# A vision tower kernel on one core: three matmul groups and two element-wise steps change their place within the round

## What is computed

```python
h = einsum(patches, W)                                   # 768 -> 256, the tokens
n = layernorm(h)
x_proj = n @ in_w + in_b
mod = gelu(n @ mod_w1 + mod_b1) @ mod_w2 + mod_b2        # 256 -> 1024 -> 256
y = irfft(rfft(x_proj * mod) * rfft(kernel))             # circular convolution over the 196 tokens
h = h + y @ out_w + out_b
n = layernorm(h)
gate = top 2 of softmax(n @ router_W.T + router_b)       # 6 experts, renormalised
h = h + n @ base_W.T + base_b + (n @ A.T) @ B.T + sum_e gate_e (n @ routed_A_e.T) @ routed_B_e.T
```

## Time and profile before

| | |
|---|---|
| median of 3 runs | 1248.16 us (1247.44 to 1250.17) |
| the profiled execution | 1247.64 us |
| its span in the trace | 1245.8 us |
| PE busy | 1223.9 us (98%) |
| DVE busy | 888.8 us (71%) |
| ACT busy | 643.2 us (52%) |
| POOL busy | 406.9 us (33%) |
| granted TensorE clock | 0.999 of full speed |

### The profile page before, as it was taken

The page is one execution under the profiler, slowest core; times in us unless marked ns, Lnnn a source line. Parts: engine busy times, 40 slices in busy tenths (PEclk is TensorE's granted clock), DMA queues, the critical chain, the costliest instruction groups (busy, mean ns, idle before and its releaser), DMA issues.

```text
span 1245.8 us, 20849 instructions
## 1 busy us (share of the span) xinstructions
PE 1223.9 (98%) x7914; PEld 1175.7 (94%) x7914; DVE 888.8 (71%) x2591; ACT 643.2 (52%) x1197; POOL 406.9 (33%) x459
## 2 busy tenths in 40 slices
PE   9999999999999999999999999999999999999998
PEld 8899999999999999999999999999999999999996
DVE  6477766677766777766777666777667777667777
ACT  6645555545555445555455555455554445454432
POOL 3523244332244232343232443323442323433220
PEclk9999999999999999999999999999999999999999
DMA  7310222221322111222202222212221112211001
GB/s 244 94 49 20 68 69 68 56 34 47 69 69 68 56 28 55 69 68 56 59 23 68 69 68 56 33 49 68 68 69 55 26 57 68 68 56 33 14 13 34
DMA packets 85089, 72.97 MB, mean 59 GB/s; under 512 B 64775, under 2 KB 78958, under 8 KB 81150
## 3 DMA queue, kind: packets, MB, share of 16 engines
q1 hardware_dynamic: 84990, 71.66, 20.4%
HBM read 43.07 MB, written 12.85 MB: 45 GB/s over the span
## 4 chain that ended last, share of the span: by engine, by line
PE 80%; DVE 9%; ACT 7%; issue 2%; DMA 1%; SPq 1%; POOL 0%; ACTq 0%; DVEq 0%
PE rotating L1457 16%; PE rotating L1458 15%; PE rotating L1459 15%; PE rows_ps L1457 8%; PE rows_ps L1458 6%; PE rows_ps L1459 6%; PE turn L1744 5%; PE turn L1507 2%; PE rows_ps L1517 2%; ACT gelu_h L661 2%; DVE y_l L1161 1%; ACT y_h L698 1%; ACT gelu L656 1%; DVE gelu_l L1106 1%; DVE gated_l L1186 1%
## 5 line engine op out<-in xcount | busy, mean ns | idle before, releaser
L529 POOL TENSOR_TENSOR folded<-modulated 128x196 f32<-128x196 f32 x63 | 38.1, 605 | 565.0 <-DVE modulated L1118 565.0
L656 ACT ACTIVATE gelu<-rotating,consts 128x392 f32<-128x392 f32 x256 | 145.4, 582 | 109.2 <-PE rotating L1459 108.9
L514 POOL TENSOR_TENSOR gelu_l<-gelu,gelu_h 128x784 fp32r<-128x784 f32 x62 | 128.7, 2075 | 213.1 <-DVE norm L1101 172.0
L509 POOL TENSOR_TENSOR patches_l<-patches,patches_h 128x384 fp32r<-128x384 f32 (+1 forms) x186 | 182.1, 1008 | 2.8 <-ACT patches_h L608 2.8
L1457 PE MATMUL rotating<-x_h,w_h 128*128 128x392 f32 x512 | 177.2, 346 | 1.6 <-ACT gelu L656 1.6
L1457 PE MATMUL rotating<-gelu_h,w_h 128*128 128x392 f32 x512 | 177.4, 346 | 0.0
L1458 PE MATMUL rotating<-x_l,w_h 128*128 128x392 f32 x512 | 174.6, 341 | 0.0
L1459 PE MATMUL rotating<-x_h,w_l 128*128 128x392 f32 x512 | 174.6, 341 | 0.0
L1458 PE MATMUL rotating<-gelu_l,w_h 128*128 128x392 f32 x512 | 174.2, 340 | 0.0
L1459 PE MATMUL rotating<-gelu_h,w_l 128*128 128x392 f32 x512 | 174.0, 340 | 0.0
L1457 PE MATMUL rows_ps<-tokw_h,patches_h 128*128 128x256 f32 x570 | 162.9, 286 | 1.5 <-DVE patches_l L871 1.5
(11 more groups left out here) (300 smaller groups left out, 2997.7 us busy)
## 6 DMA issues: line engine op xcount, KB each, us to landing
patches<-dram_x_rest SPq DMA_DIRECT2D x30, 1152.0 KB, 5.2
out<-h_sb SPq DMA_DIRECT2D x30, 384.0 KB, 2.5
prod<-spec_y SPq DMA_TRANSPOSE x60, 3.2
patches<-dram_x_first SPq DMA_DIRECT2D x2, 384.0 KB, 5.7
h_sb<-dram_x_second SPq DMA_DIRECT2D x1, 768.0 KB, 7.6
patches<-dram_x_fourth SPq DMA_DIRECT2D x1, 768.0 KB, 9.6
h_sb<-dram_first SPq DMA_DIRECT2D x2, 320.0 KB, 3.5
gelu<-dram_w SPq DMA_DIRECT2D x1, 512.0 KB, 8.1
```

Of the source, the lines that this page charges most:

```text
L509: pool.tensor_tensor(patches_l[:, k, 0:n], patches[:, k, 0:n], patches_h[:, k, 0:n].bitcast(F32), ALU.subtract).then_inc(pool_patches_lo, 1)
L514: pool.tensor_tensor(gelu_l[:, 2 * j:2 * j + 2, :], gelu[:, 2 * j:2 * j + 2, :], gelu_h[:, 2 * j:2 * j + 2, :].bitcast(F32), ALU.subtract)\
L529: pool.tensor_tensor(folded[:, m, 0, :, 1:NF], fwd, back, ALU.add)
L656: act.activation(gelu[:, k, :], bank(g + 1, UP[k])[:, 0:GT], ACT.Gelu, bias=b1_bias[:, k:k + 1]).then_inc(act_gelu, 1)
```

## The change

Four edits, all of order; no instruction is added, removed or resized.

1. PE: `routed(tail)` goes from between up blocks 6 and 7 to behind up block 7.
2. ACT: `gelu_tile(mid, 5)` goes from behind `fold_hi` to ahead of `gated_hi`.
3. DVE: `gelu_lo(mid, 2)` goes from ahead of the spectral products to behind `spectrum_of_y`, where `gelu_lo(mid, 3)` follows it.
4. PE: the first of the eight blocks of `mlp_down(mid, 0)` goes from behind the mixer's products to ahead of them, with the wait for gelu 6 (`act_gelu`) that stood before it.

```diff
@@ ACT
                 gelu_tile(mid, 4)
+                gelu_tile(mid, 5)
                 if in_range(tail):
                     gated_hi(tail, bank(i, TURN_GATED))
                 if in_range(back):
                     fold_hi(back)
-                gelu_tile(mid, 5)
                 gelu_hi(mid, 1)
@@ DVE
                     finish(tail, rows_ps)
-                for j in range(0 if i == 1 else 2, 3):
-                    gelu_lo(mid, j)
                 if in_range(back):
                     real_products(back)
                     imaginary_products(back)
                     spectrum_of_y(back)
-                gelu_lo(mid, 3)
+                for j in range(0 if i == 1 else 2, 4):
+                    gelu_lo(mid, j)
@@ PE
                 mlp_up(mid, 6)
+                pe.wait_ge(act_gelu, HC * mid + 6)
+                mlp_up(mid, 7)
                 if in_range(tail):
                     routed(tail, rows_ps)
-                pe.wait_ge(act_gelu, HC * mid + 6)
-                mlp_up(mid, 7)
                 if in_range(back):
                     dft(back)
@@ PE
+                pe.wait_ge(act_gelu, HC * mid + 7)
+                mlp_down(mid, 0, (0,))
                 if in_range(back):
                     pe.wait_ge(dve_y_lo, DH * back + DH)
                     mixer_tiles(back, rows_ps[:, 2], bank(i, OUT)[:, 0:DIM])
-                pe.wait_ge(act_gelu, HC * mid + 7)
-                mlp_down(mid, 0, range(HC))
+                mlp_down(mid, 0, range(1, HC))
```

## The result

The changed kernel takes 1216.88 us (median of 4 runs, 1213.93 to 1218.77) where the kernel before takes 1248.21 us: ratio 0.9745, 95% interval 0.9718 to 0.9771. Measured again in a later session, it took 1214.24 us (1214.13 to 1214.35) against 1247.59: 0.9728 (0.9715 to 0.9742). The forecast was 1217, range 1213 to 1228. Of the four executions of the first session two took 1213.93 and 1215.07 us at a granted clock of 1.000 and 0.999 of full speed and two took 1218.68 and 1218.77 at 0.997, so that their median, 1216.88, lies between two kinds.

A forecast was written before the change was run, and what follows sets the result against it. PE, busy 98%, was taken as the bound, with three stalls a round waiting for DVE. 29 x 1.13 = 32.8 us, less 1.5, took 31.3 off 1247.64: 1216.3, plus 0.5 for the median: 1217 us, range 1213 to 1228.

The forecast's parts named there:

- 1.13 us a round: PE's late starts plus slow steps: 0.36 ahead of `routed`, 0.29 ahead of the inverse transform, 0.48 ahead of the mixer.
- the three places: Where PE waited for DVE once per round: ahead of `routed`, ahead of the inverse transform and ahead of the mixer.
- the two kinds of round: At the mixer: 12 rounds with a stall of 0.38 us, 18 with 0.54, the latter with `y_lo` in four pieces.
- The rule: A PE group starts at full pace 0.16 us behind its releaser's end or when PE comes to it, whichever is later.
- The first rival: Ahead of `dft`: `fold_l`, slowed by POOL or released 0.4 us late, makes PE wait; 10.4 us back, 1227.5 us; 12%.
- the port's order: At the SBUF port pair of DVE and POOL: the later instruction blocks; `fold_l` starts 0.7 us first, so no delay.
- The second rival: On DVE: two low parts of gelu at 1.55 us each delay `whole_y`; mixer waits 1.05 us a round, 1247 us; 7%.
- margins that would not hold: Three margins of 0.16 us or less, two about zero: half of 0.1 us a round expected lost, 1.5 us.
- the sum: The gain over the loop before any deduction: 29 rounds x 1.13 = 32.8 us, with round 2 put at 0.

The follow-up runs named there:

- the run with the high part first: The changed kernel with ACT's high part of gelus 2 and 3 moved from behind `fold_hi` to ahead of it: 1262.10 us, ratio 1.0110 to the kernel before.

## Why the prediction was right

- **The stalls and their price.** 1.13 us a round was read from PE's starts, 1.15 was gained. The part that the busy share hides, the slow first step of 0.11 us behind a wait, was real at each of the three places: the first records are back at 0.28 and 1.93 us, and undoing edit 2 gave 1.08 late plus 0.10 slow. Most of the 0.02 between 1.13 and 1.15 is the inverse transform: the one round that was read had it 0.18 late, the mean of the 29 is 0.20.
- **What is late next.** The margins were forecast as the time between a releaser's end and the group's start: `dft` 0.17, inverse transform 0.27, mixer 0.32 and 0.16 in the two kinds of round. Measured, over rounds 3 to 31: 0.16 to 0.19, 0.24 to 0.26, 0.32 to 0.33 and 0.15 to 0.17. The rule asks for 0.16, so nothing was left between two of these and a stall, and yet no group was late in any round. The prediction did not count on that: it expected some of the margins to fail. The first rival (12%), in which `dft` takes the wait over, was ruled out by the port's order, which the run with the high part first then showed from the other side.
- **The second rival**, low parts of 1.55 us that hold `whole_y` back, fell: two take 1.85 together, since POOL is idle by then, and `whole_y` starts 1.44 behind the inverse transform, which is 1.55 less the slow step.
- **The mis-sized terms are small.** I took off 1.5 us for margins that would not hold; all held, and this is the 1.5 us between the sum (1214.8 in the terms of the profiled execution) and 1216.3. In the later session 33.4 us were gained, against 32.8 in the sum before that deduction. Round 2, taken at 0, came out near it by two terms that cancel. Its `dft` starts 0.8 us late for `fold_l`, since gelu 5 is ahead of `fold_hi` there with no `routed` to gain from, which the forecast mentioned and did not price; its stalls ahead of the inverse transform and the mixer are gone. From the copy that waits for the transposing DMA (`sine_whole`, L673) to the mixer it is 17.31 us where it was 16.99, and 0.54 of that is the down block that now stands ahead of the mixer.
- **Luck.** That the forecast of 1217 lies within 0.2 us of the first median is chance. The 1.5 us taken off for margins were not lost, and that median is drawn up by the two executions at the lower clock. The later session's 1214.24 is 2.8 us below the forecast, inside its range, and nearer to the sum without the deduction.
- **The interaction** was in the working (the products' start was reckoned for edits 1 and 3 together), but the text put one price beside each edit. The runs show that this reading would be wrong for edit 1: alone it is worth nothing.

## What to carry to other kernels

Where one engine is busy 98% of the span, read its stalls from the distance between starts, group by group, and add the slow first step behind a wait. Then carry each edit along the chain to the next meeting point before pricing it: a wait that is removed ahead of another one that is itself late only moves there, and an edit that is worth nothing alone can be worth 10 us beside another. Check the order of every step that now comes earlier on its own engine, since one activation in the old place cost the gain of all four edits.

## What was not expected of the hardware

The start of the program varied from run to run: the copy of round 2 that waits for the transposing DMA began at 55.83 us in the first profiled execution of the changed kernel and at 54.86 in the later session, in the same program, and `dft` at 62.96 and 62.00 accordingly. The kernel before had the copy at 54.82. The spans of the two are 1213.3 and 1212.5.

The rest of the spread of the first session goes with the granted clock. By my estimate a clock lower by 0.003 makes 1215 us longer by 3.6 us, and the two executions at 0.997 are 3.6 to 4.8 us above the other two. Of the kernels with edit 2 undone, with the high part first and with edit 4 alone, too, the slowest execution is the one at 0.997 (1252.26, 1264.52 and 1236.70 us). Why the clock was lower in them no run shows.

Margins of 0.03 us and less held in 29 rounds of 29. In this kernel, where all these waits are between engines of one core, the rounds repeat so exactly that such margins can be used.
